# Decoding the first six blocks of NF4 weights inside the linear attention, with the LoRA factors loaded there, and the first product placed after four blocks

## The chip, the cores and the metric

The kernel runs as one program on one core of a Trainium2 chip. The metric is the device time of one execution in microseconds, the median of several executions. Three executions of the kernel before took 2260.47, 2263.17 and 2263.21 us. The execution that the profiler recorded took 2263.59 us.

## The reference

Two transformer-like blocks are applied to x (8 x 256 x 1024, f32). Each has an attention part and a feed-forward part, and all work on the same 2048 rows of 1024. The change touches the first block only:

```
x = x + tanh(g_xattn[0]) * linear_attention(layernorm(x), ctx)   # softmax of q over the 32 channels of a head, of k over 1024; q @ (k^T v)
x = x + tanh(g_ffn[0])   * nf4_ffn(layernorm(x), ...)            # NF4 weights with LoRA, below
x = x + tanh(g_xattn[1]) * autocorrelation(layernorm(x), ctx)    # by DFT products
x = x + tanh(g_ffn[1])   * dora_linear(layernorm(x), ...)

def nf4_ffn(x1, ...):                       # DM = 1024, DFF = 2752, rank 16
    def dequant4(codes, absmax):            # codes 0..15 of NF4, a scale for each 64 of them
        return NF4[codes].reshape(o, i // 64, 64) * absmax[:, :, None]
    y1 = x1 @ Wg + x1 @ g_lora_a @ g_lora_b
    y2 = x1 @ Wu + x1 @ u_lora_a @ u_lora_b
    x3 = relu(y1) * y2
    return x3 @ Wd + x3 @ d_lora_a @ d_lora_b
```

## The kernel before, in words

Four phases run one after the other, each in its own block of the program. All engines meet at the end of a block before any of them starts the next. There is no scheduler: each engine works off a list written out by hand, and semaphores (`wait_ge`, `then_inc`) order the engines against each other.

**Phase 1, linear attention.** It has 16 tiles of 128 rows. A tile goes through software-pipelined steps: in step i, ScalarE (ACT) copies the transposed exponentials of tile i out of PSUM (`ekT`, L351), waits for VectorE (DVE) to invert the sums (`rS`, L455), spreads them (`rSx`, L355), takes the exponentials of tile i+1 (`eq`, `ek`, L341, L345), normalizes tile i-1 (`xn`, L363) and copies tile i-2 out as the high half of the next phase's input (`xT_hi`, L367). Steps 16 to 18 only drain the pipeline. Behind steps 14 to 18 hangs some small work that finds the scales of the feed-forward part (`ffn_scales`, on ACT the three squares L156). SyncE (SP) issues the loads: for each tile X and ctx (512 KB each) after `ek` of the tile one step back, and ctxT (512 KB) after the product L401 of the tile two back.

**Phase 2, feed-forward with NF4 weights.** DFF is cut into 11 pairs of 2 x 128 columns. The weights of a pair are 12 units (`pack_units`) of 128 x 512: units 0 to 3 are gate and up of the first 128 columns, 4 to 7 of the second, 8 to 11 are the down weights. A unit u is made so:

- SP loads its codes (256 KB, L569) and its scales (`absm`, 2 x 128 KB, L571) into rings of three.
- ACT decodes: eight Prelu instructions in a row on one tile, each of which puts one kink into the piecewise linear curve from code to level (`decode`, L615).
- DVE multiplies by the scale (`wt<-level`, L725, counted by the semaphore `scaled`), TensorE (PE) makes the LoRA part of the unit (`lora`, L791, counted by `lora_mm`), and DVE adds it (`wt<-ps_lora`, L728, counted by `wt_done`).
- ACT rounds to f16 (`w_hi`, L621) and GpSimd (POOL) makes the f16 rest (`w_lo`, L679, counted by `wlo_done`).

`wt` and `ps_lora` have two buffers each: DVE's L725 of unit g waits for `wlo_done` >= g-1, and the LoRA product of unit g for `wt_done` >= g-1. Both factors of LoRA are split into f16 parts at the start: ACT L645 (three parts of `lora_a`) and L604 (`lora_b`), DVE L749 and L715. PE's very first LoRA product waits for all of this.

The products of a pair are `up(j, c, t)`: 48 matmuls of 512 columns for column block c and row block t (L809), in two halves, gate and up. `up` with t = 0 waits for the units of its c: the first half of `up(0, 0, 0)` for `wlo_done` >= 2, the second for 4. ACT `relu` (L630) and DVE `mul` (L738) take each product out of PSUM, and `up` number n waits for `mul` of number n-2. The work of a pair stands in 12 slots. Each slot makes one unit that lies `AHEAD` = 6 units ahead, so that before slot 0 of pair 0 six units are made with nothing beside them:

```
for u in range(AHEAD):           # PE, before the loop over pairs
    lora(0, u)
...
decode(0, 0, first=True)         # ACT, before the loop over pairs
...
for u in range(1, AHEAD):
    decode(0, u, first=u < 2)
    w_hi(0, u - 1)
w_hi(0, AHEAD - 1)
```

Phases 3 and 4 (autocorrelation, the second feed-forward) are not touched.

Of the kernel before, what the change touches and what calls it, by code (L numbers as in the profile page):

```python
# [19 lines left out]
F32 = mybir.dt.float32  # L20
# [22 lines left out]
UNITS = 12  # L43
TB = B * L // BANK
# [190 lines left out]
def phase_linear_attention(nc, io, res):  # L235
# [5 lines left out]
    X, xT_hi, xT_lo, ident, blk, tg, mhalf, gates = (res[k] for k in ("X", "xT_hi", "xT_lo", "ident", "blk", "tg", "mhalf", "gates"))  # L241
    x_d = io["x"].rearrange("b (h p) n -> b h p n", p=P)
    c_d = io["ctx"].rearrange("b (h p) n -> b h p n", p=P)
    with ExitStack() as ctx:
# [40 lines left out]
        with nc.Block() as block:  # L285
            @block.sync
            def _(sp):
# [48 lines left out]
            def _(act):  # L336
# [144 lines left out]
def phase_nf4_ffn(nc, io, res):  # L481
# [10 lines left out]
    AHEAD = 6  # L492
# [3 lines left out]
    with ExitStack() as ctx:  # L496
# [18 lines left out]
        LROWS = 96  # L515
        lora_a = sb("lora_a", [LROWS, 3, D], HALF)
        lora_bf = sb("lora_bf", [LROWS, 3, PAIR])
# [10 lines left out]
        la_in, la_hi, la_done = sem("la_in"), sem("la_hi"), sem("la_done")  # L528
        lb_in, lb_hi, lb_done = sem("lb_in"), sem("lb_hi"), sem("lb_done")
        kink_done = sem("kink_done")  # L530
# [29 lines left out]
        with nc.Block() as block:  # L560
            @block.sync
            def _(sp):
                def load(j, u, first=False):
# [10 lines left out]
                def load_lora(j, first=False):  # L574
                    if not first:
                        sp.wait_ge(lb_done, j)
                    sp.dma_start(lora_bf[:], io["lora_b"][j]).then_inc(lb_in, 16)

                load(0, 0, first=True)
                for m in range(3):  # L580
                    sp.dma_start(la_f[m], io["lora_a"][:, m]).then_inc(la_in, 16)
                load_lora(0, first=True)
                for u in range(1, UNITS):
                    load(0, u, first=u < RING)
# [1057 lines left out]
```

## Time and profile before

| | |
|---|---|
| three executions | 2260.47, 2263.17, 2263.21 us |
| the profiled execution: its time, its span | 2263.59 us, 2261.8 us |
| granted TensorE clock, mean of the span | 0.981 |
| PE busy | 2146.1 us, 95% of the span |
| ACT busy | 1159.8 us, 51% |
| DVE busy | 1112.7 us, 49% |
| phase 1 | from 0 to about 181 us |
| phase 2 until the first product `up` | from about 181 to 220 us |

The span is the time from the first to the last instruction. The rest of the execution's time, 1.8 us, lies outside of it. Times in the views count from the span's start.

### The profile page before, as it was taken

To read this page: it belongs to the slowest core of one execution; us is meant where nothing else is said; L and a number is where in the kernel's file an instruction comes from. 1 tells how busy PE (TensorE), PEld (TensorE's weight loads), DVE (VectorE), ACT (ScalarE), POOL (GpSimd) and SP (SyncE) were. 2 spreads that over 40 slices of the span, in tenths; PEclk is the share of its full clock that TensorE was granted. 3 is DMA by queue.
4 is the path that set the end of the run, shared out by engine and by line. 5 is a ranking of instruction groups with operands and counts; after the bars stand their busy time and mean duration, and the time that the engine had idled before them with its cause. 6 is when DMAs were issued, how large, how long until landed. Compare 5 with 4: busy or idle time off the path is not lost. (4 is left out here: it accounts for less than half of the span.)

```text
span 2261.8 us, 26372 instructions
## 1 busy us (share of the span) xinstructions
PE 2146.1 (95%) x10050; PEld 1071.7 (47%) x10050; DVE 1112.7 (49%) x2047; ACT 1159.8 (51%) x1827; POOL 426.5 (19%) x448
## 2 busy tenths in 40 slices
PE   6882999999999999999999999999799999988999
PEld 5761444444444444444444444444355555544444
DVE  6883242342525242442525242434577777756443
ACT  5667656656565656656565666554233343324221
POOL 1111211112121211112121211111132223321000
PEclk9995999999999999999999999999999999999999
DMA  5433111121111111111111111111200000000111
GB/s 193 163 116 103 59 54 55 47 62 47 47 62 47 52 57 52 47 61 47 49 59 47 53 55 53 47 56 66 93 19 19 19 19 19 19 0 2 50 49 49
DMA packets 55373, 125.51 MB, mean 55 GB/s; under 512 B 8336, under 2 KB 8720, under 8 KB 55120
## 3 DMA queue, kind: packets, MB, share of 16 engines
q1 hardware_dynamic: 55248, 123.84, 16.8%
q8 instruction: 79, 1.29, 0.2%
q14 instruction: 46, 0.38, 0.1%
HBM read 115.42 MB, written 8.39 MB: 55 GB/s over the span
## 5 line engine op out<-in xcount | busy, mean ns | idle before, releaser
L615 ACT ACTIVATE level<-level 128x512 f32<-128x512 f32 x924 | 581.8, 630 | 29.3
L809 PE MATMUL ps_ring<-xT_hi,gu_hi 128*128 128x512 f16 x1376 | 522.9, 380 | 2.8 <-DVE rel L736 2.8
L809 PE MATMUL ps_ring<-xT_lo,gu_hi 128*128 128x512 f16 x1376 | 522.7, 380 | 0.0
L809 PE MATMUL ps_ring<-xT_hi,gu_lo 128*128 128x512 f16 x1376 | 522.5, 380 | 0.0
L725 DVE SCALAR_TENSOR_TENSOR wt<-level,w_scale,absm 128x512 f32<-128x512 f32 x132 | 98.9, 749 | 496.9 <-ACT level L615 496.9
L744 DVE SCALAR_TENSOR_TENSOR X<-ps_ring,ffn_gain,X 128x512 f32<-128x512 f32 x352 | 260.3, 749 | 138.1 <-PE ps_ring L832 138.0
L832 PE MATMUL ps_ring<-dn_hi,hid_hi 128*128 128x512 f16 x704 | 266.9, 379 | 0.0
L832 PE MATMUL ps_ring<-dn_hi,hid_lo 128*128 128x512 f16 x704 | 266.8, 379 | 0.0
L832 PE MATMUL ps_ring<-dn_lo,hid_hi 128*128 128x512 f16 x672 | 254.7, 379 | 0.0
L679 POOL TENSOR_TENSOR gu_lo<-wt,gu_hi 128x512 f16<-128x512 f32 x88 | 102.7, 1167 | 766.8 <-ACT gu_hi L621 766.8
L809 PEld LDWEIGHTS ps_ring<-xT_hi,gu_lo 128*128 128x128 f16 x1376 | 134.6, 98 | 163.4 <-issue 1.4
L809 PEld LDWEIGHTS ps_ring<-xT_hi,gu_hi 128*128 128x128 f16 x1376 | 134.8, 98 | 161.6 <-DVE rel L736 3.3
L809 PEld LDWEIGHTS ps_ring<-xT_lo,gu_hi 128*128 128x128 f16 x1376 | 134.9, 98 | 158.2 <-issue 1.1
L630 ACT ACTIVATE rel<-ps_ring 128x512 f32<-128x512 f32 x84 | 50.1, 597 | 291.5 <-PE ps_ring L809 291.5
L738 DVE SCALAR_TENSOR_TENSOR rel<-ps_ring,hid_gain,rel 128x512 f32<-128x512 f32 x84 | 63.1, 751 | 204.0 <-ACT rel L630 204.0
L621 ACT ACTIVATE gu_hi<-wt 128x512 f16<-128x512 f32 x88 | 55.0, 625 | 176.0 <-DVE wt L728 176.0
L679 POOL TENSOR_TENSOR dn_lo<-wt,dn_hi 128x512 f16<-128x512 f32 x42 | 48.6, 1157 | 348.9 <-ACT dn_hi L621 348.9
L1065 PE MATMUL a_ps<-xT_hi 128*128 128x512 f32 x256 | 112.5, 592 | 1.4 <-PEq L560 1.4
L832 PEld LDWEIGHTS ps_ring<-dn_hi,hid_lo 128*128 128x128 f16 x704 | 68.8, 98 | 83.2
L832 PEld LDWEIGHTS ps_ring<-dn_hi,hid_hi 128*128 128x128 f16 x704 | 68.8, 98 | 78.4
L728 DVE SCALAR_TENSOR_TENSOR wt<-ps_lora,lora_gain,wt 128x512 f32<-128x512 f32 x132 | 99.2, 751 | 4.7
L832 PEld LDWEIGHTS ps_ring<-dn_lo,hid_hi 128*128 128x128 f16 x672 | 65.8, 98 | 74.6
(205 smaller groups left out, 2836.2 us busy)
## 6 DMA issues: line engine op xcount, KB each, us to landing
codes<-in_codes SPq DMA_DIRECT2D x132, 256.0 KB, 2.8
absm<-in_absmax SPq DMA_DIRECT2D x264, 128.0 KB, 3.1
X<-in_x SPq DMA_DIRECT2D x16, 512.0 KB, 4.5
c_in<-in_ctx SPq DMA_DIRECT2D x16, 512.0 KB, 5.6
cT<-in_ctxT SPq DMA_DIRECT2D x16, 512.0 KB, 3.5
xT_hi<-in_ctx SPq DMA_DIRECT2D x8, 1024.0 KB, 4.9
out<-X SPq DMA_DIRECT2D x16, 512.0 KB, 2.6
w<-in_w SPq DMA_DIRECT2D x1, 4096.0 KB, 14.0
```

Source lines behind the costliest of these rows:

```text
L615: act.activation(level[u % 2][:], codes[u % RING][:] if k == 0 else level[u % 2][:], ACT.Prelu, bias=bias, scale=scale, alpha=alpha).then_ ...
L621: act.activation(dest(u, 0), wt[u % 2][:], ACT.Copy).then_inc(whi_done, 1)
L630: act.activation(rel[t % 2][:], ps_ring[2 + 2 * (t % 2)][:], ACT.Relu).then_inc(rel_done, 1)
L679: pool.tensor_tensor(dest(u, 1), wt[u % 2][:], dest(u, 0), ALU.subtract).then_inc(wlo_done, 1)
L725: dve.scalar_tensor_tensor(wt[u % 2][:], level[u % 2][:], w_scale[:, m:m + 1], absm[u % RING][:], ALU.mult, ALU.mult).then_inc(scaled, 1)
L728: dve.scalar_tensor_tensor(wt[u % 2][:], ps_lora[u % 2][:], lora_gain[:, m:m + 1], wt[u % 2][:], ALU.mult, ALU.add).then_inc(wt_done, 1)
L738: dve.scalar_tensor_tensor(rel[t % 2][:], ps_ring[3 + 2 * (t % 2)][:], hid_gain[:], rel[t % 2][:], ALU.mult, ALU.mult).then_inc(mul_done, 1)
L744: dve.scalar_tensor_tensor(dst, ps_ring[n % 6][:], ffn_gain[:], dst, ALU.mult, ALU.add).then_inc(acc_done, 1)
L809: mm = pe.matmul(o[:], w[c][:, m, k, :], xx[:, k, ts], start=(q == 0), stop=(q == 3 * KD - 1))
L832: mm = pe.matmul(ps_ring[n % 6][:], hh[c][:, i * P:(i + 1) * P], w[c][:, hf * BANK:(hf + 1) * BANK], start=(q == 0), stop=(q == len(split) ...
L1065: mm = pe.matmul(ps[pair][:, half], fwd[:, t, kind - 2, 0 if half is re else 1, :], src(t), start=(t == 0), stop=(t == 1))
```

## The change

Six tiles `first[0..5]` of 128 x 512 and tiles for the LoRA factors (`la_f`, `lora_bf`) are kept from phase 1 on. In phase 1, SP loads the codes of units 0 to 2 right after the first loads, those of units 3 to 5 before the loads of batch 3, and the LoRA factors before those of batch 5. ACT runs the kinks there, in place: in each of the steps 1 to 16 one kink of three units, between `ekT` and `rSx` (`first_kinks`). Units 0 to 2 take steps 1 to 8, units 3 to 5 take steps 9 to 16. In phase 2 the decoding of these six units and the loads of their codes are gone; three of the tiles become the ring of codes and two the level tiles of the later units. PE's list changes too: four LoRA products stand ahead of `up(0, 0, 0)`, and those of units 4, 5 and 6 behind it. ACT's list rounds all six units (`w_hi`) before it decodes unit 6. The diff, cut to its core:

```diff
@@ phase_linear_attention, sync
+                for u in range(AHEAD // 2):
+                    sp.dma_start(res["first"][u][:].bitcast(I32), io["codes"][0, u]).then_inc(res["first_in"], 16)
                 for b in range(1, B):
+                    if b == 3:
+                        for u in range(AHEAD // 2, AHEAD):
+                            sp.dma_start(res["first"][u][:].bitcast(I32), io["codes"][0, u]).then_inc(res["first_in"], 16)
+                    if b == 5:
+                        sp.dma_start(res["la_f"][:], io["lora_a"]).then_inc(res["la_in"], 16)
+                        sp.dma_start(res["lora_bf"][:], io["lora_b"][0]).then_inc(res["lb_in"], 16)
@@ phase_linear_attention, scalar
+                def first_kinks(i):
+
+                    turn, k = divmod(i - 1, len(kinks))
+                    if 0 <= turn < 2:
+                        scale, bias, alpha = kinks[k]
+                        act.wait_ge(res["first_in"], 16 * (AHEAD // 2) * (turn + 1))
+                        if k:
+                            act.wait_ge(res["kink_done"], AHEAD // 2 * (i - 1))
+                        for u in range(AHEAD // 2 * turn, AHEAD // 2 * (turn + 1)):
+                            block_u = res["first"][u][:]
+                            act.activation(block_u, block_u if k else block_u.bitcast(I32), ACT.Prelu, bias=bias, scale=scale, alpha=alpha).then_inc(res["kink_done"], 1)
+
                         act.activation(ekT[h][:], psE[:], ACT.Copy).then_inc(ekT_done, 1)
+                    first_kinks(i)
+                    if exists(i):
                         after(act, rS_mm, i)
@@ phase_nf4_ffn
-        codes = [sb(f"codes{s}", [P, BANK], I32) for s in range(RING)]
+        first = res["first"]
+        codes = [t[:].bitcast(I32) for t in first[AHEAD - RING:AHEAD]]
-        level = [sb(f"level{s}", [P, BANK]) for s in range(2)]
+        level = first[0:2]
-        la_f = [t[0:LROWS].bitcast(F32) for t in (hid_hi[0], hid_hi[1], hid_lo[0])]
+        la_f = [res["la_f"][:, m] for m in range(3)]
@@ phase_nf4_ffn, sync: load
-                    if not first:
-
+                    if g >= RING:
                         sp.wait_ge(scaled, g - RING + 1)
-                    sp.dma_start(codes[s][:], io["codes"][j, u]).then_inc(codes_in[s], 16)
+                    if g >= AHEAD:
+                        sp.dma_start(codes[s], io["codes"][j, u]).then_inc(codes_in[s], 16)
@@ phase_nf4_ffn, scalar
-                decode(0, 0, first=True)
-                act.wait_ge(la_in, 48)
+                act.wait_ge(la_in, 16)
                 for m in range(3):
                     act.activation(lora_a[:, m], la_f[m], ACT.Copy, scale=ab_scale[0:LROWS, 0:1]).then_inc(la_hi, 1)
                 lora_parts(0)
-                for u in range(1, AHEAD):
-                    decode(0, u, first=u < 2)
-                    w_hi(0, u - 1)
-                w_hi(0, AHEAD - 1)
+                for u in range(AHEAD):
+                    w_hi(0, u)
@@ phase_nf4_ffn, tensor
-                for u in range(AHEAD):
+                for u in range(4):
                     lora(0, u)
 
                 def pair(j, more):
                     for k, unit in slots(j, more):
+                        if j == 0 and k == 0:
+                            up(0, 0, 0)
+                            for u in range(4, AHEAD + 1):
+                                lora(0, u)
+                            continue
```

The lists of the engines show what this moves. A row is line, operation, out<-in and shape; xN counts equal instructions that stand together. First PE's list at the start of phase 2, before:

```order
L774 UNCONDITIONAL_BRANCH
L791 MATMUL ps_lora<-lora_b,lora_a 128x128 x28
L809 MATMUL ps_ring<-xT_hi,gu_hi 128x512
L809 MATMUL ps_ring<-xT_lo,gu_hi 128x512
L809 MATMUL ps_ring<-xT_hi,gu_lo 128x512
...
L791 MATMUL ps_lora<-lora_b,lora_a 128x128 x4
```

And of the change (line numbers are those of its own file; L806 and L824 are the L791 and L809 of before):

```order
L789 UNCONDITIONAL_BRANCH
L806 MATMUL ps_lora<-lora_b,lora_a 128x128 x16
L824 MATMUL ps_ring<-xT_hi,gu_hi 128x512
L824 MATMUL ps_ring<-xT_lo,gu_hi 128x512
L824 MATMUL ps_ring<-xT_hi,gu_lo 128x512
...
L806 MATMUL ps_lora<-lora_b,lora_a 128x128 x16
```

The 28 small matmuls of seven units ahead of the first product are now 16, of four units. Behind the first product's 48 matmuls (cut here) stand 16 (units 4 to 7) where there were 4 (unit 7). Next ACT's list at the same place, before:

```order
L598 UNCONDITIONAL_BRANCH
L615 ACTIVATE level<-codes 128x512
L615 ACTIVATE level<-level 128x512 x7
L645 ACTIVATE lora_a<-hid_hi,ab_scale 96x1024 x2
L645 ACTIVATE lora_a<-hid_lo,ab_scale 96x1024
L604 ACTIVATE lora_b<-lora_bf,ab_scale 96x768
L615 ACTIVATE level<-codes 128x512
L615 ACTIVATE level<-level 128x512 x7
L621 ACTIVATE gu_hi<-wt 128x512
```

And of the change:

```order
L617 UNCONDITIONAL_BRANCH
L661 ACTIVATE lora_a<-la_f,ab_scale 96x1024 x3
L623 ACTIVATE lora_b<-lora_bf,ab_scale 96x768
L638 ACTIVATE gu_hi<-wt 128x512 x6
L632 ACTIVATE first<-first 128x512 x8
L647 ACTIVATE rel<-ps_ring 128x512
L638 ACTIVATE gu_hi<-wt 128x512
L657 ACTIVATE hid_hi<-rel 128x512
```

No decoding stands ahead of the six roundings any more. The first eight kinks of phase 2 are unit 6's. Last, one step of ACT's list in phase 1 of the change, from `ekT` to the next `ekT`:

```order
L374 ACTIVATE ekT<-psE 128x1024
L368 ACTIVATE first<-first 128x512 x3
L380 ACTIVATE rSx<-rS 128x1024
L352 ACTIVATE eq<-X,nmr,rstd 128x1024
L356 ACTIVATE ek,ksum<-c_in,ncm 128x1024
L388 ACTIVATE xn<-X,nmr,rstd 128x1024
L392 ACTIVATE xT_hi<-psX 128x8x128
L374 ACTIVATE ekT<-psE 128x1024
```

Before, `rSx` stood right behind `ekT`. The whole list of ACT has one ACT_TABLE_LOAD, at its second row, in both programs. In SP's list the five LoRA and code loads stand where the diff puts them, and the loads of phase 2 begin with six of `absm`.

## Rows read from the trace of the kernel before

**Rows 1.** Busy time by stage: us, each engine's busy time (instructions), granted clock, DMA share, GB/s.
```profile
181.00:220.00 39.00, 3.86 (x29) 2.58 (x30) 12.19 (x14) 32.43 (x51) 5.18 (x4) 0.50 0.48 133
220.00:320.00 100.00, 100.00 (x475) 45.67 (x474) 29.46 (x39) 67.45 (x112) 21.81 (x19) 0.99 0.20 61
```

**Rows 2.** Timeline, phase 2's start: start, us, engine, line, out<-in [idle before <-releaser].
```profile
179.52 1.23 DVE L448 SCALAR_TENSOR_TENSOR xT_lo<-psX,xT_hi 128x1024 f16<-128x1024 f32 x1 [0.81 <-ACT xT_hi L367]
181.03 0.33 SPq L569 DMA_DIRECT2D codes<-in_codes  x1
...
191.65 2.19 ACT L645 ACTIVATE lora_a<-hid_hi,ab_scale 96x1024 f16<-96x1024 f32 x2 [2.45 <-DMA hid_lo<-in_lora_a]
...
197.57 0.75 DVE L725 SCALAR_TENSOR_TENSOR wt<-level,w_scale,absm 128x512 f32<-128x512 f32 x1
...
198.39 0.75 DVE L728 SCALAR_TENSOR_TENSOR wt<-ps_lora,lora_gain,wt 128x512 f32<-128x512 f32 x1
```

**Rows 3.** Timeline, units 2 to 4 on ACT, DVE, POOL and PE, to the first product.
```profile
212.61 0.61 ACT L615 ACTIVATE level<-codes 128x512 f32<-128x512 int32 x1
212.78 1.30 POOL L679 TENSOR_TENSOR gu_lo<-wt,gu_hi 128x512 f16<-128x512 f32 x1 [4.37 <-ACT gu_hi L621]
...
217.76 0.61 ACT L621 ACTIVATE gu_hi<-wt 128x512 f16<-128x512 f32 x1
...
218.77 0.75 DVE L728 SCALAR_TENSOR_TENSOR wt<-ps_lora,lora_gain,wt 128x512 f32<-128x512 f32 x1
...
219.58 0.61 PE L791 MATMUL ps_lora<-lora_b,lora_a 96*128 96x128 f16 x4 [5.06 <-DVE wt L728]
...
219.98 0.63 PE L809 MATMUL ps_ring<-xT_hi,gu_hi 128*128 128x512 f16 x1
```

**Rows 4.** Timeline, end of the first product and what follows it.
```profile
225.23 0.63 ACT L621 ACTIVATE gu_hi<-wt 128x512 f16<-128x512 f32 x1 [1.18 <-DVE wt L728]
225.76 0.61 ACT L615 ACTIVATE level<-codes 128x512 f32<-128x512 int32 x1
...
231.65 0.39 PE L791 MATMUL ps_lora<-lora_b,lora_a 96*128 96x128 f16 x4
...
231.87 0.38 PE L809 MATMUL ps_ring<-xT_hi,gu_hi 128*128 128x512 f16 x1
```

**Rows 5.** Timeline of ACT in phase 1: steps 1, 9 and 15, and the drain.
```profile
22.97 1.06 ACT L355 ACTIVATE rSx<-rS 128x1024 f32<-128x1024 f32 x1 [1.22 <-DVE rS L455]
...
101.50 1.06 ACT L355 ACTIVATE rSx<-rS 128x1024 f32<-128x1024 f32 x1 [2.73 <-DVE rS L455]
...
159.04 1.05 ACT L355 ACTIVATE rSx<-rS 128x1024 f32<-128x1024 f32 x1
...
172.77 1.24 ACT L363 ACTIVATE xn<-X,nmr,rstd 128x1024 f32<-128x1024 f32 x1 [7.56 <-issue]
```

**Rows 6.** Waits of ACT in phase 1: who for whom, us in total, times, longest.
```profile
ACT rSx L355 <- DVE rS L455: 34.1, 15, 2.7
```

**Rows 7.** SP's issues of one step, and the statistics on the loaded tile.
```profile
94.89 0.33 SPq L306 DMA_DIRECT2D X<-in_x  x1
...
106.61 0.68 DVE L424 BATCH_NORM_STATS2 st<-X 128x6 f32<-128x512 f32 x1
```

**Rows 8.** DMA issues 88 to 108 us: count, KB, us to landing.
```profile
X<-in_x SPq DMA_DIRECT2D x2, 512.0 KB, 4.7
```

**Rows 9.** Groups on ACT over the whole span: the table load.
```profile
L341 ACT ACT_TABLE_LOAD x1 | 1.3, 1283 | 7.7 <-DVE nmr L432 7.7
```

**Rows 10.** Busy time by short stage around PE's clock changes, columns as in rows 1.
```profile
168.00:170.00 2.00, 1.44 (x11) 1.08 (x12) 1.85 (x3) 0.00 (x0) 0.00 (x0) 1.00 0.00 0
170.00:172.00 2.00, 0.26 (x2) 0.17 (x2) 1.25 (x3) 0.00 (x0) 0.32 (x2) 0.85 0.00 0
219.90:222.50 2.60, 2.60 (x9) 0.99 (x8) 0.00 (x0) 2.47 (x5) 0.00 (x0) 0.50 0.52 193
222.50:232.00 9.50, 9.50 (x48) 4.46 (x47) 2.33 (x4) 7.22 (x13) 2.46 (x2) 0.99 0.18 55
```

More of the change, by code:

```diff
@@ L43 @@
 UNITS = 12
+AHEAD = 6
+LROWS = 96
 TB = B * L // BANK
@@ L241, in phase_linear_attention @@
     X, xT_hi, xT_lo, ident, blk, tg, mhalf, gates = (res[k] for k in ("X", "xT_hi", "xT_lo", "ident", "blk", "tg", "mhalf", "gates"))
+    kinks = nf4_kinks()
     x_d = io["x"].rearrange("b (h p) n -> b h p n", p=P)
@@ L491, in phase_nf4_ffn @@
     HID_FIRST = 2
-    AHEAD = 6
     UPS = 2 * TB
@@ L562, in _, with load @@
             def _(sp):
-                def load(j, u, first=False):
+                def load(j, u):
                     g = unit_no(j, u)
                     s = u % RING
-                    if not first:
+                    if g >= RING:
                         sp.wait_ge(scaled, g - RING + 1)
-                    sp.dma_start(codes[s][:], io["codes"][j, u]).then_inc(codes_in[s], 16)
+                    if g >= AHEAD:
+                        sp.dma_start(codes[s], io["codes"][j, u]).then_inc(codes_in[s], 16)
                     for half in range(2):
@@ L572, in load, with load_lora @@
                                      io["absmax"][j, u, half].partition_broadcast(QBLK)).then_inc(absm_in[s], 16)
-                def load_lora(j, first=False):
-                    if not first:
-                        sp.wait_ge(lb_done, j)
+                def load_lora(j):
+                    sp.wait_ge(lb_done, j)
                     sp.dma_start(lora_bf[:], io["lora_b"][j]).then_inc(lb_in, 16)
[L579 to L584, printed above, removed]
+                for u in range(UNITS):
+                    load(0, u)
                 for j in range(1, PAIRS):
@@ L604, in lora_parts, with decode @@
                     act.activation(lora_b[:], lora_bf[:], ACT.Copy, scale=ab_scale[0:LROWS, 1:2]).then_inc(lb_hi, 1)
-                def decode(j, u, first=False):
+                def decode(j, u):
                     g = unit_no(j, u)
-                    act.wait_ge(codes_in[u % RING], (j * (UNITS // RING) + u // RING) * 16 + 16)
-                    if not first:
-                        act.wait_ge(scaled, g - 1)
+                    act.wait_ge(codes_in[u % RING], ((g - AHEAD) // RING) * 16 + 16)
+                    act.wait_ge(scaled, g - 1)
                     for k, (scale, bias, alpha) in enumerate(kinks):
@@ L614, in decode @@
                             act.wait_ge(kink_done, g * NK + k)
-                        act.activation(level[u % 2][:], codes[u % RING][:] if k == 0 else level[u % 2][:], ACT.Prelu,
+                        act.activation(level[u % 2][:], codes[u % RING] if k == 0 else level[u % 2][:], ACT.Prelu,
                                        bias=bias, scale=scale, alpha=alpha).then_inc(kink_done, 1)
@@ L724, in weights @@
                     dve.wait_ge(kink_done, g * NK + NK)
-                    dve.scalar_tensor_tensor(wt[u % 2][:], level[u % 2][:], w_scale[:, m:m + 1], absm[u % RING][:], ALU.mult, ALU.mult).then_inc(scaled, 1)
+                    source = res["first"][u] if g < AHEAD else level[u % 2]
+                    dve.scalar_tensor_tensor(wt[u % 2][:], source[:], w_scale[:, m:m + 1], absm[u % RING][:], ALU.mult, ALU.mult).then_inc(scaled, 1)
                     dve.wait_ge(scaled, g + 1)
@@ L1549, in build @@
         res["const_in"] = ctx.enter_context(nc.semaphore("a_const_in"))
+        for name in ("first_in", "kink_done", "la_in", "lb_in"):
+            res[name] = ctx.enter_context(nc.semaphore(name))
         res["ctx_in"] = [ctx.enter_context(nc.semaphore(f"a_ctx_in{s}")) for s in range(2)]
@@ L1552, in build @@
             res["xT_lo"] = inner.enter_context(nc.sbuf_tensor("xT_lo", [P, KD, B * L], HALF))
+            res["first"] = [inner.enter_context(nc.sbuf_tensor(f"first{u}", [P, BANK], F32)) for u in range(AHEAD)]
+            res["la_f"] = inner.enter_context(nc.sbuf_tensor("la_f", [LROWS, 3, D], F32))
+            res["lora_bf"] = inner.enter_context(nc.sbuf_tensor("lora_bf", [LROWS, 3, PAIR], F32))
             phase_linear_attention(nc, io, res)
```

9 lines of the change are left out of this document (4 added, 5 removed).

## The prediction

> **What bounds the kernel now.** I read the busy time by stage first. From 220 us on PE is busy without a gap and ACT only two thirds of the time [rows 1]. From 181 to 220 us PE is busy for 3.9 us of 39 while ACT is busy for 32.4. So at the start of phase 2 nothing but ACT's list sets the time, and every microsecond by which the first product comes earlier there moves all that follows, since PE is the bound behind it. The timeline then says what this start is made of. Phase 1's last instruction ends at 180.75 and SP issues 0.3 us later [rows 2]. ACT decodes unit 0, splits the LoRA factors from 191.65 on, and PE's first LoRA product and DVE's first scaling follow about 6 us later [rows 2]. From there each unit costs one decoding (212.61 to 217.76, 5.15 us) plus its rounding, until unit 4 is weighted at 219.52 and PE's last LoRA product and the first of the big ones start at 219.58 and 219.98 [rows 3]. At the other end I looked for room in phase 1. ACT waits there before `rSx` for DVE's `rS`, 34.1 us in 15 steps [rows 6], 1.22 us in step 1 and 2.73 in step 9, but nothing in step 15 [rows 5].
>
> **The kinks in phase 1.** 48 Prelu instructions are added, three a step. Two instructions that don't depend on each other start 0.53 us apart on ACT (225.23 and 225.76, each some 0.62 long [rows 4]), and the three kinks of a step belong to three units. So a step gets 3 x 0.53 = 1.6 us, or 1.9 if each waited out its 0.63. The change puts them exactly where ACT waits. Step 0 has none of them, and its own wait (15 waits, of which steps 1 to 14 take 14) can't be above 2.73, so the 14 steps wait at least (34.1 - 2.7) / 14 = 2.2 us on the mean. That covers 1.6 and also 1.9. Step 1 has only 1.22: `rSx` there comes 0.3 to 0.7 us late, once. Step 15 has no wait: `rSx` moves from 159.04 to 160.6, PE's transposes behind it by about the same, less what PE was itself late. I take 0.15 us for both together, with 0 and 2.3 (0.7 + 1.6, nothing absorbed) as the bounds. In step 16 ACT sits idle for 7.56 us before `xn` [rows 5], which hides its three.
>
> **The loads in phase 1.** The first three blocks of codes (0.77 MB) queue behind the first tiles and are wanted only in step 1. Batch 3 gets 0.77 MB more, batch 5 gets lora_a and lora_b, 1.47 MB. Step by step SP issues X at 94.89, it lands 4.7 us later [rows 7, 8], and the statistics read it at 106.61 [rows 7]: 7.0 us of room. SP itself loses 0.4 us for each of the added issues, in time in which it waits for `ek`. What runs ahead of X at batch 5 takes, at the 0.52 MB in 4.7 us that such a landing shows, 13 us. At the start of phase 2 the DMA engines moved 133 GB/s in 0.48 of their time [rows 1], so 277 GB/s while they worked, which makes 5.3 us. A step is (159.04 - 101.50) / 6 = 9.6 us long [rows 5] and its own 1.57 MB would not fit into it at the first rate (14 us), so I take the second: hidden, cost 0. The upper bound is 13 - 7 = 6 us, once. The codes of batch 3 are about half of that, and hidden at either rate.
>
> **The start of phase 2.** The offsets are those of before, without decoding.
> - ACT starts on `lora_a` when the phase starts, at 181.05, not at 191.65. DVE's first scaling keeps its distance of 5.92 us (191.65 to 197.57 [rows 2]): 186.97. The six `absm` issues from 181.03 on are done by then.
> - DVE needs 0.82 + 0.75 = 1.57 us for a unit (197.57, 198.39 [rows 2]). Units 0 and 1 are weighted at 188.5 and 190.2. Rounding of unit 1 takes 0.61 and the rest on POOL 1.30, with 0.1 between them (217.76, 212.78 [rows 3]): `wlo_done` is 2 at 192.2 and PE starts `up(0, 0, 0)` at 192.3. Unit 2 waits on `wlo_done` of unit 0 and unit 3 on that of unit 1, so units come 3.6 us apart in twos: unit 3 is complete at 192.3 + 1.6 + 2.0 = 195.9. PE's first half lasts longer than that, since 24 matmuls at even the fast pace take 5.2 us (231.65 - 219.98 = 11.67 us for all 48, in which the first 2.6 us are at 0.50 clock [rows 4, 10]).
> - So the first product moves from 219.98 to 192.3: 27.7 us gained.
> - Behind it PE has units 4 to 7. Unit 4's LoRA product is readable 0.4 us after its start, DVE adds it in 0.75, only then may unit 6's run (`wt_done` >= 5), and only after another 0.82 + 0.75 unit 7's (`wt_done` >= 6). Then the second product starts: 0.4 + 0.75 + 0.07 + 1.57 + 0.1 + 0.22 = 3.1 us after the end of the first, where it was 0.22 (231.65 to 231.87 [rows 4]). 2.9 us are given back.
> - What is late next? ACT rounds unit 5 and begins to decode unit 6 about 3.5 us after the first product's end, where before it was 6 us ahead of that end. Decoding takes 5.15, scaling and LoRA 1.57, `mul` of the first product 0.75: 11.0 us after the first product's end. The third product needs that `mul`, and PE reaches it at 3.1 + 48 x 0.2155 = 13.4 us. It is in time by 2.4 us. From then on ACT gains on PE, since it is busy only 67 us of 100 [rows 1].
>
> **The sum.** 2263.6 (the profiled execution) - 27.7 + 2.9 + 0.15 = 2239.0 us. That execution lies 0.4 us above the median of the three shown, which is less than they differ among themselves (2.7 us), so I leave 2239 as the forecast. A measurement of this kernel can tell about 0.2% (4.5 us) from no change.
>
> **Rivals.**
> 1. *The clock falls in the wait behind the first product.* PE now waits 2.4 us there in two pieces, with small matmuls between. In the trace PE's clock was full from 168 to 170 us and fell in the next two, in which PE worked 0.26 us (mean 0.85); the first product started at 0.50 and ran so for 2.6 us [rows 10]. Against it: the wait behind the first product comes after 9 us of dense work at 0.99. If it falls, the second product pays as the first does, 2.6 us at half pace, 1.3 us lost: 2240.3. The Trainium skill ("TensorE: Matmul & The Clock Gate", HAM oscillation — how this bites in real kernels) speaks against the change's order here: a wait for operands between bursts of matmuls throttles the array, and the next burst starts cold.
> 2. *The transfers at batch 5 are late.* DVE stands for up to 6 us, once: 2241 to 2245.
> 3. *ACT's kinks stretch each step of phase 1.* The step of 9.6 us is a loop through ACT, PE and DVE. If what ACT waits for is itself moved by ACT, the wait doesn't hide the kinks but moves along. At half of 1.6 us in 14 steps: 11 us, 2250. For it: DVE and PE have little slack in a step. Against it: ACT's wait is for DVE alone, and neither `ekT` nor what DVE does before `rS` stands behind the kinks.
> 4. *The other side: ACT changes its function table.* Exp and Prelu now alternate in each step. If they lay in different tables, a step would pay two loads of 1.28 us [rows 9]: 2.57 + 1.6 - 2.2 = 2.0 us beyond the wait, in the 14 steps with a wait 28 us, and 4.2 in step 15: 2239 + 32 = 2271, slower. It decides from about 1.7 us a step on, where the 24.6 us of gain are eaten. Against it: the trace has a single load in its whole span, at the first Exp [rows 9], although Prelu runs later (212.61 [rows 3]), and the built list of the change has one as well. The Trainium skill ("ScalarE: Activation LUTs", Table sets: the hidden batching unit) says to batch calls by table set and not by function, and doesn't list Prelu. By its figure for a switch, 2.66 us, an estimate of this case is 2 x 2.66 x 16 = 85 us on ACT, some 2300.
>
> **How the numbers follow.** The sum as worked out has 0.80, rival 1 0.06, rival 2 0.06, rival 3 0.05 and rival 4 0.02; 0.01 is left for a wait that I don't see and that eats everything. The range for 8 in 10 goes from 2235.5 (the executions' own spread of 2.7, and a start that is a microsecond quicker) to 2243.0 (step 15's 1.6 us unabsorbed, the clock, and part of a late transfer). Faster by over 0.2% holds in the sum and in rivals 1, 2 and 3: 0.97. The same: 0.01. Slower: 0.02.
>
> **What the changed kernel's profile would show.** ACT's wait before `rSx` falls from 2.2 to 0.6 us a step and the steps keep their 9.6 us; phase 1 still ends at 180.8 to 181.1. No wait for X or ctx around batch 5. The first LoRA product at 187.1, the first `up` at 192.3, a gap of 3.1 us before the second with `wt` as what PE waits for, and PE at 0.99 clock in it; no PE wait in front of the third. It would be wrong if phase 1 ends later than 182, if `absm` or something else delays units 2 and 3 so that the first product's second half stalls, or if ACT's late decoding reaches the third product.

## The result, and the profile after

| | before | change |
|---|---|---|
| median of 4 runs (lowest to highest), us | 2263.19 (2260.47 to 2266.53) | 2238.47 (2236.95 to 2239.41) |
| ratio | | 0.9894, 95% interval 0.9882 to 0.9905 |
| profiled execution: time / span, us | 2263.6 / 2261.8 | 2239.3 / 2237.5 |
| mean granted clock of TensorE | 0.981 | 0.987 |

The change takes 24.7 us off; the prediction said 2239.0. In two later comparisons (e0_same, e10_same_again) the same kernel took 20.2 and 21.5 us less than the kernel before, and its twelve executions have a mean of 2239.8. The busy time by stage of the changed kernel (us, busy time and instructions of PE, PEld, DVE, ACT and POOL, granted clock, DMA share, GB/s) answers to [rows 1].

```profile
160.00:183.80 23.80, 11.61 (x62) 7.89 (x60) 16.92 (x46) 11.32 (x15) 3.86 (x5) 0.80 0.00 0
183.80:195.20 11.40, 2.25 (x17) 1.51 (x18) 9.22 (x11) 5.67 (x7) 2.67 (x2) 0.50 0.34 116
195.20:208.00 12.80, 12.39 (x56) 5.46 (x56) 2.64 (x4) 0.90 (x2) 2.57 (x2) 0.89 0.37 104
208.00:220.00 12.00, 10.66 (x55) 5.07 (x56) 3.80 (x6) 9.39 (x16) 4.41 (x4) 1.00 0.29 89
220.00:320.00 100.00, 100.00 (x483) 46.01 (x481) 40.26 (x55) 66.55 (x110) 19.58 (x18) 1.00 0.18 56
```

The stage without a product is now 11.4 us long, where it was 39, and DVE has taken ACT's place in it: 9.2 of 11.4 us. The timeline of the start of phase 2 in the changed kernel, as [rows 2 and 3] for before:

```profile
182.33 1.23 DVE L473 SCALAR_TENSOR_TENSOR xT_lo<-psX,xT_hi 128x1024 f16<-128x1024 f32 x1 [0.81 <-ACT xT_hi L392]
183.84 11.31 SPq L595 DMA_DIRECT2D absm<-in_absmax  x12
183.85 3.23 ACT L661 ACTIVATE lora_a<-la_f,ab_scale 96x1024 f16<-96x1024 f32 x3 [1.64 <-PEq L288]
...
189.77 0.75 DVE L740 SCALAR_TENSOR_TENSOR wt<-first,w_scale,absm 128x512 f32<-128x512 f32 x1
...
189.89 1.01 PE L806 MATMUL ps_lora<-lora_b,lora_a 96*128 96x128 f16 x8 [8.82 <-DVE lora_b L729]
...
195.18 0.59 PE L824 MATMUL ps_ring<-xT_hi,gu_hi 128*128 128x512 f16 x1 [1.73 <-POOL gu_lo L693]
```

The phase starts at 183.84 here and at 181.03 in [rows 2]; where those 2.8 us are from comes below. Counted from the phase's start, the first scaling is at 5.93, the first LoRA product at 6.05 and the first big product at 11.34. Before, that product came at 38.95. The end of the first product and what follows it, as [rows 4]:

```profile
206.98 0.61 PE L806 MATMUL ps_lora<-lora_b,lora_a 96*128 96x128 f16 x8
...
208.29 0.40 PE L806 MATMUL ps_lora<-lora_b,lora_a 96*128 96x128 f16 x4 [0.69 <-DVE wt L743]
...
209.73 0.40 PE L806 MATMUL ps_lora<-lora_b,lora_a 96*128 96x128 f16 x4 [1.05 <-DVE wt L743]
...
209.97 0.38 PE L824 MATMUL ps_ring<-xT_hi,gu_hi 128*128 128x512 f16 x1
...
217.08 0.74 DVE L753 SCALAR_TENSOR_TENSOR rel<-ps_ring,hid_gain,rel 128x512 f32<-128x512 f32 x1
...
220.33 0.38 PE L802 MATMUL ps_lora<-lora_a,lora_b 96*128 96x512 f16 x1
```

PE waits twice for `wt`, as forecast; the second product starts 14.79 us after the first (11.89 before). The `mul` of the first product (`rel<-ps_ring`) ends at 217.82, 10.8 us after that product's end. PE comes to the LoRA matmul that stands ahead of the third product at 220.33, and waits neither for it nor for the product.

Phase 1: ACT's timeline in step 9 (as [rows 5]), its waits for DVE (as [rows 6]), and the only table load of the span (as [rows 9]):

```profile
101.40 1.66 ACT L368 ACTIVATE first<-first 128x512 f32<-128x512 int32 x3
...
104.24 1.05 ACT L380 ACTIVATE rSx<-rS 128x1024 f32<-128x1024 f32 x1 [1.18 <-DVE rS L480]
```

```profile
ACT rSx L380 <- DVE rS L480: 14.6, 14, 2.8
```

```profile
L352 ACT ACT_TABLE_LOAD x1 | 1.3, 1283 | 7.6 <-DVE nmr L457 7.6
```

The three kinks take 1.66 us and come out of ACT's wait (34.1 us before, 14.6 now, 1.04 a step). The steps keep their length, 9.62 us. At batch 5, the timeline of SP and DVE and the landing of X (as [rows 7, 8]):

```profile
88.01 0.35 SPq L317 DMA_DIRECT2D X<-in_x  x1
...
99.39 1.28 DVE L449 BATCH_NORM_STATS2 st<-X 128x6 f32<-128x512 f32 x2
```

```profile
X<-in_x SPq DMA_DIRECT2D x1, 512.0 KB, 10.0
```

X landed at 98.0, 10.0 us after its issue (predicted 4.7 + 5.3), and DVE reads it at 99.39: hidden, with 1.4 us to spare.

**The 2.8 us by which phase 2 starts later.** Two places in the timeline account for nearly all of it. The 16 matmuls of `psB` in step 0 took 3.62 us (from 13.18) where those of before took 2.52 (from 13.21), 1.1 us; and those of step 2 took 3.68 where those of before took 2.05 (from 29.76), 1.6 us. First the later of these PE rows of the changed kernel, then its windows around both places (columns as above):

```profile
30.83 3.68 PE L413 MATMUL psB<-blk,eq 128*128 128x128 f32 x16 [1.05 <-DVE eq L495]
```

```profile
14.00:16.00 2.00, 2.00 (x12) 2.00 (x11) 0.00 (x0) 0.45 (x1) 0.00 (x0) 1.00 0.85 315
28.00:30.00 2.00, 1.09 (x8) 0.86 (x8) 1.01 (x5) 0.24 (x1) 0.79 (x2) 1.00 0.82 256
30.00:32.00 2.00, 1.17 (x5) 1.17 (x6) 1.97 (x3) 2.00 (x3) 0.00 (x0) 0.72 1.00 387
32.00:34.00 2.00, 2.00 (x12) 2.00 (x11) 1.59 (x5) 1.47 (x3) 0.79 (x2) 0.50 0.35 143
34.00:36.00 2.00, 2.00 (x7) 1.11 (x7) 0.36 (x1) 1.00 (x1) 0.00 (x0) 0.93 0.00 0
```

The first of these windows in the kernel before:

```profile
14.00:16.00 2.00, 2.00 (x18) 2.00 (x17) 0.23 (x1) 0.48 (x1) 0.00 (x0) 1.00 0.76 307
```

In step 2 the granted clock says it: 0.50, which is 1.2 GHz in place of 2.4. In step 0 the row reads 1.00, but the pace is the same, 12 matmuls in 2 us where before had 18 in the same window; no kink has run by then, and in e0_same, the same program, these matmuls took 2.62 us. So neither place is the work of the kinks.

Behind the second product the difference between the two traces settles at 21.9 us and stays there to the last scaling of phase 2 (`wt<-level` at 1550.10 before, `wt<-first` at 1528.20 in the change). That is 27.6 us from the earlier product, less 2.9 given back behind it, less 2.8 of phase 1's end. Another 1.7 us come from a low stretch of the clock in the kernel before (0.73 and 0.85 from 1552 to 1560 us), which this execution of the change hasn't. The last 0.7 us of the 24.3 between the two spans arise behind 1594 us, in phases 3 and 4, where both traces have such stretches at different places (in the change for instance 0.50 from 1604.5 to 1611.3).

### The profile page after: what moved, and what is told of

It is laid out like the page before. It is cut to its first block and busy times, and to the rows that moved or that the text cites. A ratio compares the mean times of both kernels' runs of the same rounds, so it can differ in the third digit from the quotient of the medians.

```text
span 2237.5 us, 26380 instructions
## 1 busy us (share of the span) xinstructions
PE 2148.3 (96%) x10050; PEld 1074.2 (48%) x10050; DVE 1112.4 (50%) x2047; ACT 1156.2 (52%) x1827; POOL 426.9 (19%) x448
## 5 line engine op out<-in xcount | busy, mean ns | idle before, releaser
L632 ACT ACTIVATE first<-first 128x512 f32<-128x512 int32 x1008 | 633.1, 628 | 28.0
L824 PE MATMUL ps_ring<-xT_hi,gu_hi 128*128 128x512 f16 x1376 | 522.2, 380 | 4.6 <-DVE rel L751 2.8
L824 PE MATMUL ps_ring<-xT_hi,gu_lo 128*128 128x512 f16 x1376 | 521.9, 379 | 0.0
L824 PE MATMUL ps_ring<-xT_lo,gu_hi 128*128 128x512 f16 x1376 | 521.9, 379 | 0.0
L740 DVE SCALAR_TENSOR_TENSOR wt<-first,w_scale,absm 128x512 f32<-128x512 f32 x132 | 98.9, 749 | 479.8 <-ACT first L632 478.7
L824 PEld LDWEIGHTS ps_ring<-xT_hi,gu_hi 128*128 128x128 f16 x1376 | 134.6, 98 | 163.1 <-DVE rel L751 3.3
L824 PEld LDWEIGHTS ps_ring<-xT_hi,gu_lo 128*128 128x128 f16 x1376 | 134.5, 98 | 163.0 <-issue 0.8
L824 PEld LDWEIGHTS ps_ring<-xT_lo,gu_hi 128*128 128x128 f16 x1376 | 134.7, 98 | 157.8 <-issue 0.5
```

The lines of the kernel that those rows point to most:

```text
L632: act.activation(level[u % 2][:], codes[u % RING] if k == 0 else level[u % 2][:], ACT.Prelu, bias=bias, scale=scale, alpha=alpha).then_inc ...
L740: dve.scalar_tensor_tensor(wt[u % 2][:], source[:], w_scale[:, m:m + 1], absm[u % RING][:], ALU.mult, ALU.mult).then_inc(scaled, 1)
L824: mm = pe.matmul(o[:], w[c][:, m, k, :], xx[:, k, ts], start=(q == 0), stop=(q == 3 * KD - 1))
```

## The experiments

Times are medians in us with lowest to highest, ratios are to the kernel before on the same chip. In the traces I compare offsets from the first issue of `absm` in phase 2: for before (181.41) the second product comes at 50.46, for the change (183.84) the first at 11.34 and the second at 26.13. "Slow matmuls" are those of the first product at the 1.2 GHz pace (0.43 us apart, not 0.2155); each costs 0.21 us. The executions of the changed kernel differ among themselves by 5.4 us (2236.6 to 2242.1), so the medians of two versions tell little below that, and the offsets in a trace tell more.

**e0_same: the change once more, unchanged.**

> The changed kernel once more, for the size of what differs between two executions of one program. In the recorded execution phase 1 ended 2.8 us later than before. Theory A: 2.7 us of that are two stretches in which PE ran at its low clock (the ramp in step 0, and one at 31 to 35 us), not the kinks. Then this execution ends phase 1 somewhere else, at about 181 us if no such stretch falls into it, and the first product starts 11.3 us after the phase whatever it is. Theory B: the kinks and loads cost 2.8 us, and the phase ends at 183.5 us again, with the same steps late. Time by both 2236 to 2240 us.

2241.74 (2236.64 to 2242.07), ratio 0.9907 (0.9893 to 0.9922), span 2234.8. Without a slow stretch in phase 1 here, phase 2 starts at 181.19, 0.16 us later than SP's first issue in [rows 2]. That is what the kinks and loads cost by this trace, against 0.15 predicted. Step 15's `rSx` moved from 159.04 to 160.75, 1.7 us, but it left nothing: `ekT` of that step, which stands ahead of its kinks, was 0.15 us late already (158.29, 158.14 before). The 0.15 had built up before, 0.05 in step 0, where no kink stands, and some 0.01 a step. First and second product at 11.34 and 26.12.

**e1_old_order: only PE's list as before, all else as in the change.**

```diff
-                for u in range(4):
+                for u in range(AHEAD):
...
-                        if j == 0 and k == 0:
-                            up(0, 0, 0)
-                            for u in range(4, AHEAD + 1):
-                                lora(0, u)
-                            continue
```

> The change without its new order on PE: the LoRA products of all six units and of unit 6 stand ahead of the first product again, the kinks and loads stay in phase 1. Theory A: units now come 1.8 us apart, unit 4 is weighted 3.2 us after PE would have started, so the first product starts 3.7 us later, but the second follows at once (0.22 us): 0.8 to 0.9 us slower than the changed kernel, which is nearly nothing. Rival: the new order is what brings the first product forward, and without it 3 us and more are lost.

2238.26 (2236.87 to 2239.75), ratio 0.9894 (0.9881 to 0.9908). The first product comes at 15.02, 3.7 us later, but the second at 26.89, only 0.77 later. With the decoding gone, the new order of PE is worth 0.8 us: the earlier start is given back as the wait for units 4 to 6. The medians (2238.26 here, 2238.47 to 2241.74 of the change) can't show so little.

**e2_order_alone: the same lines of PE's order put into the kernel before.**

> The kernel before with the new order on PE alone: four LoRA products, the first product, then units 4 to 6. All six units are still decoded at the start of phase 2. Theory A: the first half starts when unit 1 is ready (208.4 us), the second when unit 3 is (219.8), the first product ends at 225.1 and the second starts at 228.2 instead of 231.9: 3.6 us faster than before. Rival: the units 4 and 5, which now come after it, cost as much as the product gains: no change. In neither does it come near the 24 us of the whole.

2263.98 (11 runs) against 2262.44 (15 runs), ratio 1.0007 (0.9998 to 1.0015). In the trace the second product comes at 47.65, 2.8 us earlier (3.6 expected). Between the halves of its first product PE waits 3.33 us for unit 3, and soon after it the clock falls, for eight matmuls (1.7 us):

```profile
220.11 0.39 PE L809 MATMUL ps_ring<-xT_hi,gu_hi 128*128 128x512 f16 x1 [3.33 <-POOL gu_lo L679]
```

```profile
219.00:220.90 1.90, 0.79 (x4) 0.41 (x5) 0.04 (x1) 1.80 (x4) 1.05 (x1) 1.00 0.35 63
220.90:224.40 3.50, 3.50 (x11) 1.22 (x8) 0.00 (x0) 2.80 (x5) 0.00 (x0) 0.51 0.32 116
```

Of the 2.8 us, the profiled span kept 1.7 us (2260.1 against 2261.8; its phase 1 ended 0.9 later) and the median nothing. Why the median shows none of it stays open. What is shown is that the order alone gives no gain that these times can measure.

**e3_lora_late: the LoRA factors are loaded at the start of phase 2, as before.**

```diff
-                    if b == 5:
-                        sp.dma_start(res["la_f"][:], io["lora_a"]).then_inc(res["la_in"], 16)
-                        sp.dma_start(res["lora_bf"][:], io["lora_b"][0]).then_inc(res["lb_in"], 16)
...
-                for u in range(UNITS):
+                load(0, 0)
+                sp.dma_start(res["la_f"][:], io["lora_a"]).then_inc(la_in, 16)
+                sp.dma_start(lora_bf[:], io["lora_b"][0]).then_inc(lb_in, 16)
+                for u in range(1, UNITS):
```

> The change with the LoRA factors loaded at the start of phase 2, after the first absm, and not in phase 1. The kinks stay in phase 1. Theory A: 1.47 MB at the rate of that stage take some 5.3 us, and with issue and landing ACT splits lora_a 7.5 us later; all of it stands ahead of the first product: 6 to 9 us slower than the changed kernel. Rival: the batch 5 of phase 1, without these loads, gives back what they cost there, and the difference is below 3 us.

2249.64 (2248.46 to 2250.92), ratio 0.9945 (0.9932 to 0.9957). The first LoRA product comes at 15.7 instead of 6.05. ACT's waits of this kernel, then PE's timeline:

```profile
ACT lora_a L661 <- DMA la_f<-in_lora_a: 11.3, 1, 11.3
```

```profile
197.14 1.01 PE L806 MATMUL ps_lora<-lora_b,lora_a 96*128 96x128 f16 x8 [18.48 <-DVE lora_b L729]
```

The transfer of 1.15 MB took 8.4 us from its issue, and the first big product comes 9.7 us later than in the change. So 9.7 us of the start depend on the early loads: of the 27.6 us some two thirds are the decoding, one third the loads.

**e4_kinks_twice: each step of phase 1 runs its three kinks and then three idle ones (slope 1) on the same tiles.**

```diff
...
+                        act.wait_ge(res["kink_done"], AHEAD // 2 * i)
+                        for u in range(AHEAD // 2 * turn, AHEAD // 2 * (turn + 1)):
+                            block_u = res["first"][u][:]
+                            act.activation(block_u, block_u, ACT.Prelu, scale=1.0, alpha=1.0).then_inc(res["again"], 1)
```

> Behind each step's three kinks stand three more Prelu instructions with slope 1 and no shift, in place, which leave the levels as they are: 6 in a step. Theory A (the wait for rS covers the kinks until it is used up): ACT has 3.3 us of them against a wait of 2.4, each of 13 steps gets 0.9 us longer, step 1 2 and step 15 1.6: phase 1 14 to 17 us longer than in the changed kernel, 2253 to 2256 us. Theory B (the wait moves along with ACT, so that part of each kink already stretches a step): the second three cost as the first three did, a constant share of 1.7 us; were it all, phase 1 would be 25 us longer. Theory C (ACT is off the path, there is more room than its wait shows): below 5 us.

2242.21 (2240.98 to 2243.79), ratio 0.9912 (0.9897 to 0.9927). The steps stayed at 9.61 to 9.62 us. Phase 2 starts at 184.22, 3.0 later than in e0_same. Of that, 1.1 us arose in step 0, ahead of any kink, where `psB` ran slowly until 16.96 (15.78 in e0_same), and 1.9 in step 15, where ACT has no wait, and behind it. What step 1 lost (its `rSx` came 2.9 us late) was made good: `ekT` stays 1.1 to 1.2 us late from step 1 to step 15. Ten steps of the change (e0_same), then ten of e4_kinks_twice, by windows:

```profile
52.00:148.00 96.00, 84.62 (x600) 69.71 (x599) 82.61 (x159) 78.86 (x100) 15.84 (x40) 1.00 0.57 185
```

```profile
55.00:151.00 96.00, 84.83 (x598) 69.52 (x597) 82.66 (x161) 94.58 (x130) 15.79 (x40) 1.00 0.56 183
```

ACT (the fourth pair of numbers) rose from 78.9 to 94.6 of 96 us and no other engine noticed. The doubled kinks did not cost 14 to 17 us: the wait before `rSx` is not all the room that there is.

This trace shows one thing more. PE's list in phase 2 is that of the change, with the same waits of 0.69 and 1.05 us behind the first product, and here the clock falls as the second product starts:

```profile
210.00:211.80 1.80, 0.54 (x7) 0.38 (x8) 1.56 (x3) 0.80 (x2) 0.91 (x1) 1.00 0.00 0
211.80:215.20 3.40, 3.40 (x12) 1.34 (x11) 0.00 (x0) 3.27 (x6) 1.40 (x2) 0.50 0.55 154
```

Eight of its matmuls ran at the slow pace, 1.7 us.

**e9_kinks_thrice: the same with six idle kinks a step.**

> Nine Prelu a step, the three kinks and six that leave the levels as they are, all ahead of rSx. With six, the steps kept their 9.6 us although ACT's wait for rS was used up: rSx came 0.9 us later than rS, PE 0.7 us later, and DVE's next use of what PE makes there lies another 1.7 us behind. Theory A (the room is ACT's 2.4 us plus these 1.7, 4.1 in all): nine take 5.0 us, each of 13 to 14 steps gets 0.9 us longer, step 1 and 15 some 2 each: 12 to 17 us longer than the change, 2251 to 2256 us. Theory B (the room ends with the 3.3 us of six): each step gets 1.7 longer, 24 us and more. Theory C: still no step longer.

2265.03 (2263.58 to 2266.01), ratio 1.0013 (1.0004 to 1.0023). The step is now 11.12 us, 1.5 longer, and phase 2 starts at 208.07. Windows of this kernel in that stretch, and its ACT timeline from one `ekT` to `rSx`:

```profile
80.00:147.00 67.00, 51.60 (x354) 44.20 (x353) 51.27 (x97) 65.96 (x96) 9.47 (x24) 0.95 0.49 164
```

```profile
100.66 1.01 ACT L382 ACTIVATE ekT<-psE 128x1024 f32<-128x1024 f32 x1
101.57 1.66 ACT L369 ACTIVATE first<-first 128x512 f32<-128x512 f32 x3
103.26 3.37 ACT L376 ACTIVATE first<-first 128x512 f32<-128x512 f32 x6
106.54 1.04 ACT L388 ACTIVATE rSx<-rS 128x1024 f32<-128x1024 f32 x1
```

ACT is busy for 65.96 of 67 us and has no wait left in most steps. Its step of 11.12 us is the sum of its own work: 4.97 us from the first kink to `rSx` (101.57 to 106.54) and 6.15 for the rest. So the room in a step of 9.61 us is 3.46 us, all of ACT's idle time, not the 2.2 to 2.7 in front of `rSx`; three kinks use 1.6 and six use 3.3.

**e5_kinks_behind: the three kinks stand behind `rSx`, ahead of `eq`, not in ACT's wait.**

```diff
-                    first_kinks(i)
...
                         act.activation(...)   # rSx
+                    first_kinks(i)
```

> The same three kinks a step, but behind rSx, ahead of the exponentials, instead of ahead of rSx. ACT does the same work. Theory A (the place matters: ahead of rSx there are 2.4 us in which ACT waits for DVE, behind rSx comes ek, for which PE waits in every step): PE's transposes come 1.6 us later, of which the 0.7 us that PE waits for DVE behind them can absorb a part, a step gets about 0.9 us longer, phase 1 some 12 us, 2250 us (between 7 and 22 us longer). Theory C (ACT has the room anywhere in its step): phase 1 ends within 1 us of the change's.

2243.05 (2240.90 to 2248.68), ratio 0.9924 (0.9907 to 0.9941). Phase 2 starts at 185.21, 4.0 later than in e0_same. `ekT` is 0.4 us late from step 1 on (step 0's slow matmuls, ahead of any kink), 2.9 us in step 6 and 4.0 in step 14. Between steps 3 and 6 lies a slow stretch of the clock, by these windows:

```profile
50.00:52.00 2.00, 2.00 (x12) 2.00 (x11) 1.83 (x6) 1.72 (x2) 0.79 (x2) 0.50 0.90 301
52.00:56.00 4.00, 4.00 (x22) 3.04 (x22) 2.35 (x4) 2.11 (x4) 0.00 (x0) 0.88 0.33 128
```

How much of the 2.5 us between those steps is the clock's and how much the kinks' is not separated. Behind step 6 the delay grows by 0.3 us in every second step, 1.2 us in all. So the place counts, but little: 0.15 us a step, at most 3.6 us in the phase. PE's waits for `ek` in phase 1 grew from 17.4 us (e0_same) to 33.8, while those for `eq`, which comes later too, fell from 10.7 to 1.4: mostly one wait stands in the place of another.

**e6_halves: two of the LoRA products behind the first product go between its halves.**

```diff
+                        for u in between if m == 0 else ():
+                            lora(0, u)
...
-                            up(0, 0, 0)
-                            for u in range(4, AHEAD + 1):
-                                lora(0, u)
+                            up(0, 0, 0, between=(4, 5))
+                            lora(0, AHEAD)
```

> The LoRA products of units 4 and 5 go between the gate half and the up half of the first product, that of unit 6 behind it. Theory A: the 2.9 us by which the second product is late are DVE's two units that start only with these products. DVE does them beside the second half, PE only pays the matmuls themselves, and the second product starts some 12.7 us after the first instead of 14.8: 2.1 us faster than the changed kernel. Rival: PE waits inside the product for wt_done of units 2 and 3 (it passes the middle 6.5 us after the start, they are done at 1.5), or ACT, which decodes unit 6 about 2 us earlier, sets the pace anyway: no change.

2237.12 (2235.56 to 2238.81), ratio 0.9895 (0.9878 to 0.9911). Second product at 24.76: 1.4 us earlier (2.1 expected), 2.2 with its 11 slow matmuls counted as the change's 7.

**e7_parts: `lora_b` is split first and `lora_a` in thirds, as PE needs them.**

```diff
+                lora_parts(0)
                 for m in range(3): ...   # lora_a on ACT
-                lora_parts(0)
...
+                a_parts(0)
...
+                    if u == 1:
+                        a_parts(1)
+                    if u == 3:
+                        a_parts(2)
...
-                pe.wait_ge(la_done, 3)
+                pe.wait_ge(la_done, 1)
```

> The start of phase 2 splits lora_b first, then the gate part of lora_a; the up part follows after unit 1 and the down part after unit 3, and PE waits for each part where it is used. Theory A: after the change, nothing but this chain of ACT and DVE stands ahead of the first product. DVE's first scaling comes 3.3 us after the phase starts instead of 5.9, the first product after 9.0 instead of 11.3 (DVE's 1.2 us for the up part now stand ahead of unit 2, which is not wanted for the first half): 2.3 us faster than the changed kernel. Rival: absm lands later than the factors are split (6 issues of 0.55 us, some 3 us to land), or the first product's second half now waits for unit 3: 0 to 1 us faster.

2238.24 (2234.51 to 2241.73), ratio 0.9897 (0.9882 to 0.9912). First product at 9.69 instead of 11.34 (9.0 expected; DVE now waits 0.8 us for `absm`), second at 25.63: 0.5 earlier, 1.8 with its 13 slow matmuls counted as 7.

**e8_halves_parts: both.** It adds no edit to those of e6_halves and e7_parts.

> Both of the edits: LoRA products of units 4 and 5 between the halves of the first product, and the LoRA factors split part by part. Theory A: the two lie behind each other on PE's list and add up, 4.4 us faster than the changed kernel, about 2234 us. Rival: the first product starts so early that its second half waits for unit 3 and its rest (ready 15 us after the phase starts, wanted at 15.5), and 1 to 2 us of it are lost.

2235.27 (2233.12 to 2235.67), ratio 0.9882 (0.9867 to 0.9897). Second product at 23.15: 3.0 earlier, 4.0 with its 12 slow matmuls counted as 7. The waits of 1.7 us in all behind the first product are gone.

**e10_same_again and e11_best_again: the change and e8_halves_parts once more, side by side.**

> The changed kernel once more, beside the next one on the same chip. Phase 1 ends at 181.0 us plus what stretches of low clock fall into it, the first product starts 11.3 us later, the second 26.1 later less or more 0.21 us for each matmul more or less at the low clock. 2236 to 2240 us.

> The version with both edits (LoRA products of units 4 and 5 between the halves of the first product, factors split part by part) once more, beside the changed kernel on the same chip. In its first profile the second product started 23.2 us after the phase, 3.0 before that of the change, although 12 matmuls instead of 7 ran at the low clock: 4.0 us without that. Theory A: the timed difference is 3 to 4 us, about 0.15%. Rival: the 5.6 us that the first comparison gave are real and something else is gained; or there is no difference and both were chance.

2240.36 (2239.08 to 2241.89), ratio 0.9904 (0.9889 to 0.9919), and 2235.43 (2235.17 to 2236.11), ratio 0.9882 (0.9868 to 0.9897). Over all runs, the eight executions of the version with halves and parts lie from 2233.1 to 2236.1 and the change's twelve from 2236.6 to 2242.1, with no overlap. It is the fastest version found. But not all of the 4.9 us between these two medians is the start of phase 2. In e11_best_again the first product comes at 10.81 (9.52 in e8_halves_parts; DVE waits 1.2 us for `absm`, not 0.5) and the second at 24.47, against 26.56 in e10_same_again. The last scaling of phase 2 is 1.9 us earlier (1524.67 against 1526.57), and the span 6.1 us (2233.4 against 2239.5). The other 4.2 us arise behind it: in e10_same_again the granted clock is 0.50 from 1528.2 to 1535.0, in e11_best_again it is 1.00 there. So the edits are worth 1.9 to 3.0 us by the traces. Whether they also make the later stretches of low clock rarer, or that was chance, is open.

## Why the prediction was right, point by point

The mechanism was right: decoding and loads left the start of phase 2, PE's earlier start was paid back in part, and phase 1 had room. That the sum met the median within 0.5 us is in part luck. The execution from which the sum starts had a low stretch of the clock that cost 1.7 us, the profiled one of the change had slow matmuls at two places in phase 1 that cost 2.7, and the medians of the other two comparisons lie 1.4 and 2.7 us above the forecast.

- **The start of phase 2: right.** 27.6 us gained against 27.7. Counted from the phase's start, the first LoRA product came at 6.05 (forecast 187.1 - 181.05 = 6.05) and the big one at 11.34 (11.25). The offsets of before held because the same instructions run in the same order between them; e3_lora_late shows that both parts, decoding and early loads, were needed for it.
- **The give-back: right.** 2.9 us, by the two waits on `wt`. e1_old_order adds what the prediction did not say: with this give-back the new order of PE nets 0.8 us.
- **The third product: right.** `mul` ended 10.8 us after the first product (forecast 11.0), PE came at 13.4, no wait.
- **Cost in phase 1: the size right by luck, the reason too narrow.** 0.16 us (e0_same) against 0.15. But the 0.15 was put down to steps 1 and 15, and neither left a delay; what there is built up elsewhere. And I took ACT's wait before `rSx` as the cover. e4_kinks_twice and e9_kinks_thrice show that it is the whole of ACT's idle time in a step, 3.46 us; e5_kinks_behind shows that outside the wait the kinks still cost only some 0.15 us a step. Rival 3's 0.8 us a step was therefore far too dear for where the kinks stand. The wait that is left is 1.04 us a step, not 0.6, since 2.2 was only its lower bound.
- **Loads: right.** The rate taken from [rows 1] (277 GB/s) gave 10.0 us to landing and 10.0 was measured; the other rate would have given 17.7.
- **"Phase 1 still ends at 180.8 to 181.1": not so in the execution shown.** Phase 2 started 2.8 us later, past the 182 that was to make the forecast wrong. The time was not lost to the change: e0_same and e10_same_again start phase 2 at 181.19 and 181.78. The size of what executions of one program differ by in phase 1 (up to 2.7 us here) was missing in that test.
- **Rival 1, the clock: not in the execution shown, but in another.** The windows from 208 to 220 show 1.00 granted with two waits of 0.69 and 1.05 us in them. With the same list and the same two waits, e4_kinks_twice lost 1.7 us to it (1.3 forecast). It is the only one of nine traces with these waits, so the rival is real, and rare in these runs. After the longer wait of 3.33 us in e2_order_alone the clock fell too. The Trainium skill ("TensorE: Matmul & The Clock Gate", HAM oscillation — how this bites in real kernels) describes bursts of matmuls that are each shorter than the wait for a DMA behind them, so that each next burst starts at the low clock. Here 1.7 us of waits stood behind 11.8 us of matmuls, so the Trainium skill spoke less plainly against the change's order than the prediction says; e4_kinks_twice shows that the clock can fall here even so. Where PE did little for long, in the 11.4 us ahead of the first product, the granted clock is 0.50; there the Trainium skill and the trace agree.
- **Rival 4, the table: did not happen.** One load of 1.28 us in the whole span, with Exp and Prelu alternating in 16 steps. The 85 us on ACT that stood for a switch of tables at every alternation did not arise either.

## What to carry to other kernels

Work that a second phase needs first can go into the idle time of a phase bound elsewhere; the room was the idle time of that engine per step (period less its own work), and the single wait seen in the trace only a part of it. An earlier start is worth what the next thing in line leaves of it: here the new order's 3.7 us of earlier first product became 0.8 at the second, while filling the wait behind it (the LoRA products between its halves) and preparing the factors in the pieces in which they are used gave 1.9 to 3.0 us more. Before a later phase end, or a time difference of a few us, is put down to a change, compare the pace of the same matmuls: it moved phase 1's end by up to 2.7 us between executions of one program, and the rest of the span by 4.2 us between two kernels that are equal from there on.

## What the runs showed of the hardware

- **Short stretches at 1.2 GHz in the middle of busy phases.** At 31 to 35 us in the change (PE busy for 1.09 and 1.17 of 2 us just before and as it fell; in e0_same it was busy for 0.94 and then 2.00 of 2 us there, and nothing fell), at 50 to 53 in e5_kinks_behind, at 1552 to 1560 in before, at 1528 to 1535 in e10_same_again. The first and the third cost 1.6 and 1.7 us. e0_same and e10_same_again, the same program as the change, have none in phase 1 from step 2 to step 15.
- **The first product after an idle start ran 6 to 14 matmuls at 1.2 GHz**: before and e1_old_order 6, the change 7, 7 and 9, e5_kinks_behind 8, e3_lora_late 9, e6_halves and e9_kinks_thrice 11, both runs of halves and parts 12, e7_parts 13, e4_kinks_twice 14. (In e2_order_alone it was 13 in the first half, and the 8 of above in the second.) That is 1.3 to 3 us lost, and takes back part of what an earlier start gains; it is one reason why e6_halves, e7_parts and e8_halves_parts gained less than was worked out.
- **The row of the granted clock can read 1.00 while matmuls run at half pace.** So it was from 14 to 16 us in the change, 12 matmuls in 2 us against 18 in before; look at the pace too.
- **DVE and POOL in each other's way.** DVE's scaling (two inputs in SBUF) took 1.53 us instead of 0.75 while POOL subtracted. The timeline of e7_parts:

```profile
189.60 1.58 POOL L693 TENSOR_TENSOR gu_lo<-wt,gu_hi 128x512 f16<-128x512 f32 x1 [0.52 <-ACT gu_hi L638]
190.20 1.53 DVE L740 SCALAR_TENSOR_TENSOR wt<-first,w_scale,absm 128x512 f32<-128x512 f32 x1
```

  In the change, `wt<-ps_lora,...` at 192.03, with one input in PSUM, kept its 0.75 us beside POOL's 1.16. The Trainium skill ("SBUF — State Buffer", SBUF: two separate sides) says that a DVE instruction with two SBUF inputs and one of GpSimd lock a shared pair of ports against each other; both rows agree with that.
